# One-core transformer block in float32: 64-row delta products, an earlier weight conversion, a rounding moved to GpSimd, and a split last store

## The reference, cut to what matters

```python
# attention step (weights only depend on codebook, weight, lora_A, lora_B)
delta      = lora_B @ lora_A * (32 / 64)          # 512 x 512, contracts 64
normalized = (weight + delta) / exp(scale_log)    # per group of 128 columns
quantized  = codebook_levels[searchsorted(thresholds, normalized)]
w_eff      = quantized * exp(scale_log) + delta
x = x + attention(x @ w_eff.T, Wqkv, bqkv, Wo, bo)
# expert step
base   = x @ W.T
gates  = top-2 softmax of (x @ Wr.T + language bias)
h      = x @ A (8 experts x 16);  y = base + 2 * (h * gates) @ B
w_ffn  = scale * (qweight - zero_point)
out    = x + y @ w_ffn.T + ffn_bias
```

## Time and profile before

| what | value |
|---|---|
| median of three runs | 107.92 us (107.66 to 108.25) |
| profiled execution | 108.04 us |
| its span, first to last instruction | 106.2 us |
| TensorE matmul, busy | 101.5 us, 96% |
| VectorE, busy | 66.3 us, 62% |
| ScalarE, busy | 51.9 us, 49% |
| GpSimd, busy | 34.3 us, 32% |
| granted TensorE clock, mean | 0.997 |

### The profile page before, as it was taken

How to read it: one execution, slowest core, us unless ns; L and a number is a source line. 1 busy time by engine, 2 the same in 40 slices (tenths; PEclk the granted TensorE clock), 3 DMA queues, 4 the chain that set the end, 5 groups by cost and what they waited for, 6 DMA issues and landing times.

```text
span 106.2 us, 1428 instructions
## 1 busy us (share of the span) xinstructions
PE 101.5 (96%) x505; PEld 83.6 (79%) x505; DVE 66.3 (62%) x157; ACT 51.9 (49%) x92; POOL 34.3 (32%) x34
## 2 busy tenths in 40 slices
PE   6899999999999999999999999999999999999980
PEld 6734588889777899899888787889898888888850
DVE  1196799999999899325999653014946802572440
ACT  4038789999999954734222238272038204002000
POOL 3000063799919993696000056400000400000000
PEclk9999999999999999999999999999999999999998
DMA  1999999960000000000000000000000540000072
GB/s 38 323 259 396 408 402 406 408 244 0 3 0 0 0 0 0 9 0 0 0 0 0 0 0 0 0 6 0 0 0 0 225 170 0 6 0 0 0 294 104
DMA packets 4455, 9.83 MB, mean 93 GB/s; under 512 B 736, under 2 KB 736, under 8 KB 4448
## 3 DMA queue, kind: packets, MB, share of 16 engines
q1 hardware_dynamic: 4304, 9.48, 24.3%
q10 hardware_dynamic: 144, 0.26, 0.8%
HBM read 7.64 MB, written 2.10 MB: 92 GB/s over the span
## 4 chain that ended last, share of the span: by engine, by line
PE 89%; DMA 4%; DVE 3%; ACT 1%; issue 0%
PE psum L860 19%; PE psum L862 19%; PE psum L861 19%; PE psum L884 7%; PE psum L876 4%; DMA lora<-in_lora 4%; PE psum L895 3%; PE psum L910 3%; PE psum L901 3%; PE psum L905 3%; PE psum L1011 2%; PE psum L1032 2%; PE psum L1026 2%; ACT moe L459 1%; PE psum L1018 1%; PE psum L928 1%
## 5 line engine op out<-in xcount | busy, mean ns | idle before, releaser
L665 DVE COPY_PREDICATED cond_work<-cond_work,psum 128x1024 f32<-128x1024 int32 x10 | 13.7, 1374 | 1.3 <-ACT cond_work L359 0.9
L860 PE MATMUL psum<-G_hi,xT_hi 128*128 128x512 f32 x32 | 12.9, 402 | 0.0
L861 PE MATMUL psum<-G_lo,xT_hi 128*128 128x512 f32 x32 | 12.5, 391 | 0.0
L862 PE MATMUL psum<-G_hi,xT_lo 128*128 128x512 f32 x32 | 12.5, 390 | 0.0
L578 POOL TENSOR_TENSOR hl<-hl,hl_bias 128x272 f32<-128x272 f32 (+2 forms) x4 | 3.1, 774 | 27.0 <-ACT hl L370 14.3
L359 ACT ACTIVATE cond_work<-cond_n,cut_bias 128x1024 f32<-128x1024 f32 x10 | 11.4, 1158 | 0.7 <-DVE cond_n L704 0.7
L520 POOL TENSOR_TENSOR xT_lo<-xT,xT_hi 128x1024 fp32r<-128x1024 f32 x4 | 9.6, 2402 | 2.4 <-DVE cond_work L671 2.4
L860 PE MATMUL psum<-xT_hi,split_b_hi 128*128 128x512 f32 x24 | 9.7, 402 | 0.0
L862 PE MATMUL psum<-xT_hi,split_b_lo 128*128 128x512 f32 x24 | 9.4, 391 | 0.0
L861 PE MATMUL psum<-xT_lo,split_b_hi 128*128 128x512 f32 x24 | 9.4, 390 | 0.0
L520 POOL TENSOR_TENSOR split_a_lo<-moe,split_a_hi 128x512 fp32r<-128x512 f32 x3 | 4.3, 1436 | 15.0 <-ACT split_a_hi L336 12.5
(11 more groups left out here) (168 smaller groups left out, 239.8 us busy)
## 6 DMA issues: line engine op xcount, KB each, us to landing
out<-cond_work SPq DMA_DIRECT2D x8, 256.0 KB, 2.1
q_i<-in_q_t SPq DMA_DIRECT2D x4, 256.0 KB, 7.5
moe<-in_moe_w SPq DMA_DIRECT2D x4, 256.0 KB, 7.5
cond_n<-in_cond_w SPq DMA_DIRECT2D x2, 512.0 KB, 7.1
xT<-in_x_t SPq DMA_DIRECT2D x2, 512.0 KB, 8.2
xT<-in_x_t SPq DMA_DIRECT2D x1, 1024.0 KB, 12.7
wqkv_n<-in_wqkv SPq DMA_DIRECT2D x1, 768.0 KB, 10.7
hlT<-in_hl_t SPq DMA_DIRECT2D x1, 272.0 KB, 6.7
```

The lines of the kernel that those rows point to most:

```text
L665: dve.copy_predicated(by_group(half(level, h)), by_group(beyond[n % len(beyond)].bitcast(I32)), psum[EARLY][:, at:at + GROUPS // 2].unsque ...
L860: pe.matmul(out_ap, l_hi, r_hi, start=first, stop=False)
L861: pe.matmul(out_ap, l_hi, r_lo, start=False, stop=False)
L862: return pe.matmul(out_ap, l_lo, r_hi, start=False, stop=last)
```

## The change

Five edits:

- Each delta product contracts 64 rows instead of 128: products 0 and 2 read partitions 0 to 63, products 1 and 3 partitions 64 to 127; the scale is no longer halved.
- `w_full(0)` on VectorE stands ahead of the threshold comparisons instead of behind `cut_bias`.
- The rounding of `moe` row block 1 goes from ScalarE to GpSimd, where it precedes `moe_rest(1)`; it has a semaphore of its own, and the counts that wait for blocks 2 and 3 are lowered by one.
- On TensorE `y_o(0)` stands ahead of `scores(1, 0)` and its wait.
- The last sequence's `y_store` and its store are made in two halves of 256 columns.

```diff
-    LORA_COPIES = 2
-    LORA_SCALE = 32.0 / 64.0 / LORA_COPIES
+    LORA_SCALE = 32.0 / 64.0
...
-            for b in range(BATCH):
+            for b in range(BATCH - 1):
                 sp.wait_ge(y_ready, b + 1)
                 sp.dma_start(out[b], y_out[:, b, :]).then_inc(stored, 16)
-            sp.wait_ge(stored, 16 * BATCH)
+            b = BATCH - 1
+            for n in range(2):
+                sp.wait_ge(y_ready, b + n + 1)
+                s = slice(n * C // 2, (n + 1) * C // 2)
+                sp.dma_start(out[b, :, s], y_out[:, b, s]).then_inc(stored, 16)
+            sp.wait_ge(stored, 16 * (BATCH + 1))
...
             beyond_cut(0, 0)
-            moe_hi(1)
             w_hi(1)
             beyond_cut(1, 0)
...
             def moe_rest(o):
-                pool.wait_ge(moe_hi_ready, o)
+                if o == 1:
+                    pool.wait_ge(moe_first_hi_ready, 1)
+                else:
+                    pool.wait_ge(moe_hi_ready, o - 1)
                 rest(split_a_lo[:, o, :], moe[:, o, :], split_a_hi[:, o, :], moe_lo_ready)
 
+            pool.wait_ge(loaded["moe1"], 16)
+            pool.tensor_copy(split_a_hi[:, 1, :], moe[:, 1, :]).then_inc(moe_first_hi_ready, 1)
             moe_rest(1)
...
+            w_full(0)
             dve.wait_ge(dve_step, cuts_at)
             keep(1, ALU.min, 3)
...
-            w_full(0)
             w_delta_first()
...
             for o in range(CT):
-                pe.matmul(psum[DELTA_BANKS[o]][:, :], lora[:, 0, o * P:(o + 1) * P], lora[:, 1, :], start=True, stop=True)\
+                rows = slice(o % 2 * RANK, (o % 2 + 1) * RANK)
+                pe.matmul(psum[DELTA_BANKS[o]][:, :], lora[rows, 0, o * P:(o + 1) * P], lora[rows, 1, :],
+                          start=True, stop=True)\
                   .then_inc(delta_done, 1)
...
             o_hl(0, 1, 2)
+            pe.wait_ge(oT_hi_ready, 1)
+            pe.wait_ge(oT_lo_ready, 1)
+            y_o(0)
             pe.wait_ge(qkvT_ready, 6)
             scores(1, 0)
-            pe.wait_ge(oT_hi_ready, 1)
-            pe.wait_ge(oT_lo_ready, 1)
-            for t in range(TPH):
+            for t in range(1, TPH):
                 y_o(t)
```

More of the change, by code:

```diff
@@ L271, in block_kernel @@
         level_late_set = sem("level_late_set")
+        moe_first_hi_ready = sem("moe_first_hi_ready")
         moe_lo_ready = sem("moe_lo_ready")
@@ L834, in gh_lo, with y_store @@
                    .then_inc(ghT_lo_ready, 1)
-            def y_store(t):
+            def y_store(t, n=slice(0, C)):
                 dve.wait_ge(y_done, t + 1)
                 dve.wait_ge(y_bias_ready, 1)
-                dve.tensor_tensor(y_out[:, t, :], psum[4 + t % 4][:, :], y_bias[:, :], ALU.add).then_inc(y_ready, 1)
+                dve.tensor_tensor(y_out[:, t, n], psum[4 + t % 4][:, n], y_bias[:, n], ALU.add).then_inc(y_ready, 1)
             softmax_max(0, 3)
@@ L852, in _ @@
             gh_lo(1, 0)
-            for t in range(TPH, BATCH):
+            for t in range(TPH, BATCH - 1):
                 y_store(t)
+            for n in range(2):
+                y_store(BATCH - 1, slice(n * C // 2, (n + 1) * C // 2))
         @block.tensor
@@ L897, in G_product @@
             def G_product(o):
-                pe.wait_ge(moe_hi_ready, o)
+                if o == 1:
+                    pe.wait_ge(moe_first_hi_ready, 1)
+                else:
+                    pe.wait_ge(moe_hi_ready, o - 1)
                 pe.wait_ge(w_hi_ready, o)
```

## The result

The change makes the kernel slower. Twenty runs of each on the same chip gave 108.02 us before (107.66 to 108.35) and 108.81 us after (107.82 to 109.16), a ratio of 1.0057 with a 95% interval of 1.0039 to 1.0075. I had forecast 107.6, 0.3% faster. The runs after lie in two groups: six from 107.82 to 108.00, fourteen from 108.59 to 109.16, with nothing between. The granted clock is 0.995 to 1.0 in all of them. (The ratios shown here leave out executions over 1.5% above the fastest of their kernel; for the kernel with the rounding alone that drops three of its late group, so its median says more.)

The account below looks back on a forecast made before the run. TensorE, with 89% of the chain, bounds the kernel, and the masks' chain is nearly as tight. -0.17 - 0.12 = -0.29 us against the profiled 108.04 gives 107.75, or 107.6 at the runs' median; range 107.0 to 108.2.

Parts of the forecast that it names:

- the part on the rounding: GpSimd rounds moe block 1 in 0.6 us; w_lo(1) and the masks' chain move by -0.17 us, bounds -0.25 and +0.51.
- my sum: Whole kernel: -0.17 us from the masks' chain and -0.12 from the last store, -0.29 us in all.
- my own sign of being wrong: TensorE shows no idle time ahead of line 905, or Bf_lo moves by more than 0.5 us either way.
- 0.40 us of room: TensorE's second pass of G_product(1): w_lo(1) ends at 15.20, the pass stands in the chain at 15.60.
- The delta: 64-row products on TensorE overlap, saving 1.28 us; only 0.32 passes the wait for w_lo(1), the rest stops at Bf_lo.
- three overlaps: Delta on TensorE: each product's second instruction runs beside the next one's first, 3 x 0.43 = 1.28 us.
- `y_o(0)` first: TensorE: three products delay scores(1, 0) by 0.69 us, but its reader starts over 2 us later: 0, bounds -0.1 and +0.1.
- The last store: Kernel's end: second half issued 0.11 us later but with half the bytes; net -0.22 to +0.2, taken as -0.12 us.
- The rival on the losing side: At moe_rest(1): GpSimd's rounding takes over 0.77 us; at 1.28 us, 108.3, or 108.5 with further slip; chance 0.12.

Follow-up runs that it names:

- the one extra wait: Kernel before, plus one more GpSimd wait, on the landing of moe block 1 ahead of moe_rest(1): 108.32 us, ratio 1.0038, 2.02 us outside the span.
- Both remedies: Changed kernel with moe_rest(2) held until w_full(2) is done and six repeated GpSimd waits removed: 107.50 us, ratio 0.9961.
- the late CAST: Kernel before, plus a late GpSimd CAST to fp32r of a 128 x 128 tile, result unused, and one wait: 108.40 us, ratio 1.0036.

## Why the prediction was wrong

**The step that failed** is in the part on the rounding: "ScalarE's freed 0.62 us gives nothing of its own ... It only waits longer." ScalarE did wait longer for `w_full(2)`, but ahead of that wait stands `moe_hi(2)`, and I left out what that releases. It ran 0.6 us sooner (14.15 instead of 14.75 us), so `moe_rest(2)` on GpSimd began at 14.85 instead of 15.44 and came ahead of `w_full(2)`, where before it had come behind. I had read the shut-out from `w_lo(1)`, and weighed it only for the GpSimd operation that met that one, `moe_rest(1)`. So the chain of masks and picks moved by +0.77 us (A), where my sum had -0.17; my own sign of being wrong, `Bf_lo` off by more than 0.5 us, came, with 0.69. Shown: undoing the edit (107.76), doing it alone (both groups), holding GpSimd back (one group, A 21.98), and loading `moe` block 2 sooner (one group, 108.95). The Trainium skill had the rule for this meeting too: "SBUF — State Buffer", Who interferes with whom, counts `tensor_scalar` among the operations that can take the shared pair, and says that issue order decides who is blocked. The trace agrees: 14.85 before 14.86, and 1.56 us instead of 0.54.

**The time outside the span** was no term of my sum. It costs 0.2 us, shown by the one extra wait. Why it depends on the length of GpSimd's list stays open.

**What held.** `w_lo(1)` ended at 14.93, where I had 15.03, behind a `moe_rest(1)` ending at 14.39 instead of 14.48; the CAST took 0.61 us, where I had 0.6; TensorE waited for `w_lo(1)` ahead of the second pass, 0.49 us where I had 0.7 to 0.9. Counted from the division by the scale, `w_lo(1)` ends 4.66 us on, instead of 4.84: 0.18 sooner, where I had 0.17. With the meeting away A is 21.94 to 22.14 in the four profiles with the rounding on GpSimd, and 22.13 to 22.21 in the seven with it on ScalarE and `moe_rest` not held; the means differ by 0.17. Two prices were off without effect. I had read 0.40 us of room ahead of the second pass from the chain; its first matmul started at 15.44 us, so there were 0.24. And from the end of `w_lo(1)` to the second pass I had 0.25; it was 0.06 (14.93 to 14.99). Both remedies together give 107.50 and 0.39% faster, where I had 107.6 and 0.3%. That is another kernel than the one I forecast, and 0.13 of it come from `y_o(0)`, which I had at 0, so the agreement is partly luck. The six early runs of the changed kernel have spans of 105.8 to 106.0 instead of 106.2, which fits the order of events that I had assumed; no profile of one of them shows it.

**The delta** was mis-sized, without effect on the time. I had three overlaps and an end at 8.1; the trace has matmuls starting in pairs, at 4.76, 5.74, 6.43 and 6.86, the two of a pair 0.00 to 0.04 us apart, and `G_first` from 7.40 (start us, us):

```profile
4.76 2.71 PE L888 MATMUL psum<-lora 64*128 64x512 f32 x8 [0.35 <-DMA lora<-in_lora]
...
7.40 3.70 PE L908 MATMUL psum<-q_i,moe 128*128 128x512 f32 x8
```

All four products of 64 rows are done in some 2.6 us instead of 4.4, twice as fast at full clock, and the switch of tiling costs at most 0.1 us (6.86 + 0.43 = 7.29, `G_first` at 7.40). The Trainium skill's concurrency of matmuls in different row groups ("TensorE: Matmul & The Clock Gate", Part 3) is what the trace bears out. Then the lead over the kernel before went, by the starts of the matmuls: 1.81 us at `G_first`, 1.47 at `x_hl(0)`, which waited for x0 (landed 11.03, began 11.17), 1.06 at the first pass of `G_product(1)`, which waited for `w_hi(1)`, 0.45 at the second, which waited for `w_lo(1)`, and 0.04 at the first pass of `G_product(2)` (17.23), which waited for `w_hi(2)`. Nothing was gained.

**`y_o(0)` first** I put at 0, bounds 0.1: it gains 0.13, by elimination. B is 70.41 to 70.46 in the seven profiles with that order and the passes of `G_product` as they were, with rounding and delta either way, and 70.55 to 70.58 in the six without it, the kernel with the late CAST (70.85) aside. In the earlier trace rows's view the scores took 1.01 us of the chain before and 0.89 after; before, they stood behind their wait for ScalarE's `q`, which `y_o(0)` now covers. No run has this edit alone.

**The last store** I put at -0.12. C is 3.09 to 3.10 with two halves and 3.14 to 3.15 with one: -0.05, its second issue behind the first on one queue, inside the bounds.

The rival on the losing side named the right edit and the wrong place: a slow copy. The copy was not slow.

## What to carry to other kernels

When work moves off an engine, follow that engine's next instructions to everything they release, up to the next wait that holds it, and look at which pairs of VectorE and GpSimd operations change their order. Where two come due within some tenths of a microsecond, the order is a toss that a load's landing decides; one more wait fixes the order, if the engine that is held has slack (here at the price of 0.2 us outside the span). Two groups of times in one kernel, at one clock, point to such a toss; only a profile shows whether a given run has it.

## What the runs showed of the hardware

- A VectorE tensor_scalar of 128 x 512 from int32 takes 0.53 to 0.55 us (0.45 at its first, early place), and 1.51 to 1.56 in the four profiles where a GpSimd tensor_tensor started 0.00 to 0.52 us ahead of it; it then ended 0.28 or 0.29 us behind GpSimd's. A two-input one takes 0.65 to 0.69 with GpSimd quiet or later than it, and 0.73 to 1.23 when it starts during such an operation: in all fourteen profiles where `w_lo(1)` did, it ended 0.55 us behind `moe_rest(1)`, however late it had started. Predicated copies, whose level comes from PSUM, stayed at 1.32 to 1.41 beside it.
- Time outside the span was 1.77 to 1.82 us with GpSimd's list at its old length (58 instructions in the trace, waits and the like counted) or shorter, 2.02 to 2.06 with one more, 2.18 and 2.19 with two more. Profiles of the span alone don't show it.
- Four fp32r products of 512 columns take 0.92 us in a stream, and 1.03 from their first start to the next pass's behind a wait.
- Four float32 products over 64 rows, on alternating halves, run two at a time: eight matmul instructions start in four pairs, the last two 0.43 us apart at full clock, where before each took 0.43 alone.
